# Two small SBUF copies per step of a decoder layer, issued by ScalarE in place of SyncE

## The chip, the cores and the metric

The kernel runs on one core of a Trainium2 chip. The metric is the device time of one execution in microseconds; the kernel before has a median of 670.93 us over 3 runs (668.68 to 674.22).

## The reference

One post-norm decoder layer in float32 on 32 sequences of 64 tokens with 256 channels. x is (32, 64, 256), the context ctx has the same shape. What is computed, cut to its core:

```python
# 1. causal self-attention, 16 heads of 16 channels, then a layer norm over the sum
qkv = einsum('bsd,od->bso', x, w_project)           # 768 outputs
att = softmax(where(causal, -1e9, q @ k.T / 4))
x   = layernorm(x + (att @ v) @ w_out.T)
# 2. cross-attention along the other axis: channels = 64, time = 256, 8 heads of 8 channels,
#    rotary positions on q and k, 256 x 256 scores for each of the 8 heads
q, k, v = Wq x + bq, Wk ctx + bk, Wv ctx + bv
p   = softmax(rope(q) @ rope(k).T / sqrt(8))
x   = layernorm(x + Wo (p @ v) + bo)
# 3. feed-forward with 8-bit activations and ternary weights, 256 -> 1024 -> 256
h   = layernorm(gelu(silu(bitlinear(x, w1, b1)))) * g + b
x   = layernorm(x + bitlinear(h, w2, b2))
```

## The kernel before, in words

Two sequences of 64 tokens fill the 128 partitions and make a pair; there are 16 pairs. Phase A (self-attention and cross-attention) is followed by two phases for the feed-forward part, which the change does not touch.

**Phase A as a pipeline.** After a prologue for the first pairs, every engine runs `body(i)` sixteen times, written out in full (bodies 0 to 15 for pairs 0 to 15). A body has 16 steps s, one for each of the 16 score tiles of pair i's cross-attention (for each of its 2 sequences 8 tiles, of two heads and one half of the 256 positions each). Beside those tiles, body i carries other pairs along: the projections and scores of self-attention of pair a = i+3, and the second half of self-attention, its norm and the rotary projections of pair j = i+2. Bodies 14 and 15 have no pair j left (`rotary` is false), bodies 13 to 15 no pair a. The order of the work on each engine is written out by hand; engines are tied together by semaphores alone.

**The cross-attention tiles.** For the softmax each row's maximum is needed before the exponential is taken. TensorE therefore computes each score tile twice: `max_head` (L531) 14 tiles ahead, for VectorE's maxima `MX` (L907), and `exp_head` (L559) with two more contraction rows that hold the negated maximum (in two bfloat16 parts), so that ScalarE's exponential `exp_tile` (L729, out `PB`) gets the difference from TensorE. The operands are `QA` and `KA`: 48 rows of q and k in three bfloat16 parts, and rows 48 and 49 of each half of `QA` for the maxima. `pv_quad` (L574) then multiplies `PB` with the values. `exp_head` of tile n waits for the exponential of tile n-2; `pv_quad` m waits for the exponentials up to 2m+1.

**How the maxima come into the rows.** For each of the two sequences b of a pair: VectorE negates the 8 tiles' maxima into `NM` (L918, L920), TensorE transposes them (`max_transpose`, L545) into a PSUM bank, ScalarE copies that to `MR` (`mt_copy`, L723), and `max_rows` (L356 to L361) waits for that copy and issues two DMAs of 4 KB from `MR` to rows 48 and 49 of the two halves of `QA` (L360). `exp_ready` makes the first `exp_head` of that sequence (tile 0 for b = 0, tile 8 for b = 1) wait for both. `mt_copy(i, 1)` stands at step 3 of body i on ScalarE, directly ahead of the exponential of tile 4 and of `pt_copy(j)`; `mt_copy(i+1, 0)` stands at step 12, ahead of `square_sum` and the exponential of tile 13. There are 32 such copies, so 64 such DMAs.

**What pair j goes through in body i.** TensorE transposes the self-attention probabilities at step 4 (`transpose_p`, L474; its bank is the one that `mt_copy` reads, so it waits for that), ScalarE copies them (`pt_copy`, L709, two instructions), TensorE multiplies with the values at step 5 (`self_pv`, L487), ScalarE copies (`ao_copy`, L716), TensorE projects at step 6 (`out_proj`, L496), VectorE and GpSimd do the layer norm (Y L869, mv L873, rs L295 and L297, X L880), TensorE projects the rotary q at step 9 (`rotary_proj("q")`, L508), VectorE rotates (L888), and GpSimd splits the result into three bfloat16 parts (`split_parts`, last operation L841).

**SyncE's queue.** SyncE (SP) issues every DMA, in this order in body i: loads of pair i+4 and i+3 (L315, L310), `max_rows(i, 1)`, `store_parts("k", j)` (the parts go to DRAM, L330) and `expand_rows("k", j)` (back into `KA` with the heads on other partitions, four DMAs, L343), the load of the context (L321), `store_parts("q", j)`, `max_rows(i+1, 0)`, `expand_rows("q", j)` into `QA`, and `cross_values(a)` (L353). `expand_rows` waits until the store has landed. `max_head` of pair i+1 begins at step 2 of body i and waits there for that pair's `expand_rows` of q and k; those were issued in the body before.

Of the kernel before, what the change touches and what calls it, by code (L numbers as in the profile page):

```python
# [39 lines left out]
HALF, HH = 64, XH // 2  # L40
ROW_M = 6 * XC
# [32 lines left out]
def build_layer(nc, x, xT, ctx, wpT, woT, xW, xB, rows, w1T, w2T, attn_tables, rotary_tables, out):  # L74
    with ExitStack() as outer:
        es = outer

        def sb(name, shape, dt=F32):
            return es.enter_context(nc.sbuf_tensor(name, shape, dt))
# [4 lines left out]
        def sem(name):  # L84
            return es.enter_context(nc.semaphore(name))

        def event(name, steps=1):
            return Event(sem(name), steps)
# [65 lines left out]
        QA = sb("QA", [P, 6, HH, D], BF16)  # L154
# [4 lines left out]
        MR = sb("MR", [32, P], BF16)  # L159
# [37 lines left out]
        mrow = [[sem(f"mrow{p}{b}") for b in range(2)] for p in range(3)]  # L197
        mx_ps, mx_red, negm = event("mx_ps", 16), event("mx_red", 16), event("negm", 4)
        mt_ps, mt_sb = event("mt_ps", 2), event("mt_sb", 2)
# [8 lines left out]
        def wait(eng, ev, pair, step):  # L208
            eng.wait_ge(ev.sem, ev.at(pair, step))  # L209
# [5 lines left out]
        def has(pair, back):  # L215

            return not isinstance(pair.v, int) or pair.v >= back
# [88 lines left out]
        def _(sp):  # L306
            def load_x(a):
                if has(a, 2):
                    wait(sp, ln1, a.plus(-2), 1)
                sp.dma_start(X[:, a.p, :], x[bass.ds(a.v, 1)].rearrange("o p d -> (o p) d")).then_inc(ld_x[a.p], 16)  # L310

            def load_xT(a):
                if has(a, 2):
                    wait(sp, vs_ps, a.plus(-2), 1)
                sp.dma_start(XT[:, a.p], xT[bass.ds(a.v, 1)].rearrange("o p k t -> (o p) k t")).then_inc(ld_xT[a.p], 16)  # L315

            def load_c(j):
                if has(j, 2):
                    wait(sp, xv_ps, j.plus(-2), 1)
                    wait(sp, ro_ps["k"], j.plus(-2), 1)  # L320
                sp.dma_start(C[:, j.p, :], ctx[bass.ds(j.v, 1)].rearrange("o p d -> (o p) d")).then_inc(ld_c[j.p], 16)  # L321

            def store_parts(n, j):

                if has(j, 2):
                    sp.wait_ge(expand[n][j.plus(-2).ring], NEXPAND * (j.plus(-2).rounds + 1))
                wait(sp, split[n], j, 5)
                dst = parts_hbm[n][j.p].rearrange("t r x -> r t x")
                for slots, parts in (((0, 2), (0, 2)), ((2, 4), (1, 3))) if n == "q" else (((0, 3), (0, 3)), ((3, 4), (1, 2))):
                    sp.dma_start(dst[:, slice(*slots)], part[n][:, slice(*parts)]).then_inc(stored[n][j.p], 16)  # L330

            def expand_rows(n, j):

                if has(j, 3):
                    wait(sp, e_ps, j.plus(-3), 16)
                sp.wait_ge(stored[n][j.p], NSTORE * (j.uses + 1))
                dst = {"q": QA, "k": KA}[n]
                for e in range(2):
                    src = parts_hbm[n][j.p].rearrange("t (e c w) x -> e c t (w x)", e=2, c=XC)[e]
                    first = src[:, 0:1].broadcast_to([XC, 3, 2 * HH * D]) if n == "q" else src[:, 0:3]  # L340
                    for g, group in enumerate((first, src[:, 1:4])):
                        low = HALF * e + 3 * XC * g
                        sp.dma_start(dst[low:low + 3 * XC, 2 * j.ring:2 * j.ring + 2].rearrange("p b h x -> p (b h x)"),  # L343
                                     group).then_inc(expand[n][j.ring], 16)

            def cross_values(a):

                if has(a, 1):
                    wait(sp, ao_ps, a.plus(-1), 1)
                wait(sp, vs_sb, a, 1)  # L350
                for b in range(2):
                    src, dst = slice(SEQ * b, SEQ * b + SEQ), slice(SEQ - SEQ * b, 2 * SEQ - SEQ * b)
                    sp.dma_start(VM[dst, b].rearrange("p (j e f) -> p j e f", e=2, f=SD)[:, :, 1 - b],  # L353
                                 VS[src, :].rearrange("p (j e f) -> p j e f", e=2, f=SD)[:, :, 1 - b]).then_inc(crossed, 16)

            def max_rows(i, b):  # L356
                wait(sp, mt_sb, i, b + 1)
                for e in range(2):
                    low = HALF * e + ROW_M
                    sp.dma_start(QA[low:low + 2, 2 * i.ring + b].rearrange("m h (u t) -> m (h u) t", u=2),  # L360
                                 MR[16 * e:16 * e + 16, :]).then_inc(mrow[i.ring][b], 16)  # L361

            p0, p1, p2 = (Pair(0, a) for a in range(3))
            sp.dma_start(wp[:], wpT.rearrange("(k p) n -> p k n", p=P)).then_inc(ld_wp, 16)
            load_xT(p0)
# [24 lines left out]
            store_parts("q", p1)  # L390
            load_c(p2)
            expand_rows("q", p1)
            max_rows(p0, 0)
            sp.dma_start(w1f[:].rearrange("p (k n) -> p k n", k=2), w1T.rearrange("(k p) n -> p k n", p=P)).then_inc(ld_ffn, 16)
            sp.dma_start(w2f[:].rearrange("p (k n) -> p k n", k=8), w2T.rearrange("(k p) n -> p k n", p=P)).then_inc(ld_ffn, 16)

            def body(i, selfs=True, rotary=True, last=False, more=True):
                if more:
                    load_xT(i.plus(4))
                if selfs:  # L400
                    load_x(i.plus(3))
                max_rows(i, 1)
                if rotary:
                    store_parts("k", i.plus(2))
                    expand_rows("k", i.plus(2))
                    if selfs:
                        load_c(i.plus(3))
                    store_parts("q", i.plus(2))
                if not last:
                    max_rows(i.plus(1), 0)  # L410
                if rotary:
                    expand_rows("q", i.plus(2))
                if selfs:
                    cross_values(i.plus(3))
# [263 lines left out]
        def _(act):  # L678
# [39 lines left out]
            def mt_copy(i, b, g):  # L718
                wait(act, mt_ps, i, b + 1)
                before = i.plus(b - 1)  # L720
                if b == 1 or has(i, 1):
                    act.wait_ge(mrow[before.ring][1 - b], NMROW * (before.rounds + 1))
                nc.scalar.activation(MR[:, :], g_b[g][0:32, 0:64].bitcast(BF16), ACT.Copy).then_inc(mt_sb.sem, 1)  # L723

            def exp_tile(i, n):
                wait(act, e_ps, i, n + 1)
                if has(i, 1) or n >= 4:
                    act.wait_ge(pv.sem, 8 * i.v + n // 2 - 1)
                nc.scalar.activation(PB[:, n % 4].rearrange("p e t -> p (e t)"), e_b[n % 2][:, :], ACT.Exp,  # L729
                                     scale=XC ** -0.5).then_inc(e_sb.sem, 1)  # L730
# [9 lines left out]
            def x_keep(a):  # L740
                wait(act, ln1, a, 6)
                nc.scalar.activation(XALL[:, bass.ds(a.v, 1), :], X1[:].unsqueeze(1), ACT.Copy).then_inc(ln1.sem, 1)
# [13 lines left out]
            p0, p1, p2 = (Pair(0, a) for a in range(3))  # L756
# [14 lines left out]
            x_keep(p1)  # L771
            self_exp(p2)
            mt_copy(p0, 0, 1)

            def body(i, first=False, selfs=True, rotary=True, last=False):
                a, j = i.plus(3), i.plus(2)
                for s in range(16):
                    exp_tile(i, s)
                    if s == 0 and not first:
                        u_copy(i.plus(-1), 1)  # L780
                    if s == 0 and selfs:
                        qk_copy(a)
                    if s == 3:
                        mt_copy(i, 1, 1)
                    if s == 4 and rotary:
                        pt_copy(j)
                    if s == 5 and rotary:
                        ao_copy(j)
                    if s == 6 and not first:
                        at_copy(act, i.plus(-1), 1)  # L790
                    if s == 8 and rotary:
                        x_keep(j)
                    if s == 8:
                        u_copy(i, 0)
                    if s == 13 and not first:
                        square_sum(act, i.plus(-1))
                    if s == 11 and selfs:
                        v_copy(a)
                    if s == 12 and not last:
                        mt_copy(i.plus(1), 0, 1)  # L800
                    if s == 15 and selfs:
                        self_exp(a)
                    if isinstance(i.v, int) and i.v == 13 and s in (7, 9):
                        weight_sum((s - 7) // 2)
                    if isinstance(i.v, int) and i.v == 14 and s in (1, 3):
                        weight_round((s - 1) // 2)
# [651 lines left out]
```

## Time and profile before

| | |
|---|---|
| Median of 3 runs | 670.93 us |
| The profiled execution | 677.3 us |
| Its span, first to last instruction | 675.4 us |
| Phase A, about | 0 to 495 us |
| Busy share TensorE / VectorE / ScalarE / GpSimd | 73% / 77% / 56% / 47% |
| Mean granted TensorE clock | 0.829 |
| `QA<-MR` | 64 DMAs of 4.0 KB, all issued by SyncE |

The page gives busy time by engine, the span in 40 slices, DMA queues, the chain that ended last, and the costliest groups of instructions. Busy shares are averages over phases with different limits. The issue of a DMA is not counted as busy on the engine that issues it, and no engine but SyncE issues any here. In a timeline, each line is the start in us, the length in us, the engine, the line of the kernel, the operation, out<-in with the shape, the count, and in square brackets the idle time of that engine just ahead of it with what ended it. PE is TensorE, PEld its weight load, DVE VectorE, ACT ScalarE, POOL GpSimd, SPq SyncE's queue.

### The profile page before, as it was taken

The page shows a single profiled execution, that of the slowest core. Times are in us where ns is not written, and L with a number is a line of the kernel's source. Part 1 is how long each engine was busy: PE and PEld are TensorE (multiplying, and loading weights), DVE is VectorE, ACT ScalarE, POOL GpSimd, SP SyncE. Part 2 cuts the span into 40 slices and gives each one's busy share as a digit, 9 for nine tenths or more (in the row PEclk, how much of TensorE's full clock was granted, in tenths as well). Part 3 has the DMA queues.
Part 4 walks back from the last instruction along what each step waited for, and adds up shares of the span by engine and source line. Part 5 has one row for each costly group of instructions (what it writes and reads, how often), then busy time and mean ns, then how long its engine had stood idle before and what let it go on. Part 6 is the DMA issues. An engine that isn't in the chain of part 4 may idle for free. (4 is left out here: it accounts for less than half of the span.)

```text
span 675.4 us, 12183 instructions
## 1 busy us (share of the span) xinstructions
PE 490.2 (73%) x3986; PEld 253.3 (38%) x4002; DVE 522.3 (77%) x1045; ACT 378.3 (56%) x681; POOL 319.9 (47%) x383
## 2 busy tenths in 40 slices
PE   5556888889888888898898888788966414545445
PEld 3332435444444344444443444333222103333333
DVE  6476678978988879889888898778437677888885
ACT  1211346555556555555565656477548958677673
POOL 6442435364464553644645537320020057776773
PEclk9787779999999999999999999878567955555555
DMA  7212522212222223132222221220000000000000
GB/s 260 59 43 74 177 67 65 68 51 74 75 65 62 64 68 83 49 76 69 72 60 66 66 77 49 51 71 4 1 0 1 0 0 8 16 16 23 16 17 32
DMA packets 51400, 37.04 MB, mean 55 GB/s; under 512 B 21392, under 2 KB 47376, under 8 KB 51216
## 3 DMA queue, kind: packets, MB, share of 16 engines
q1 hardware_dynamic: 51344, 36.33, 18.8%
q8 instruction: 31, 0.51, 0.3%
q14 instruction: 25, 0.20, 0.1%
HBM read 24.52 MB, written 10.49 MB: 52 GB/s over the span
## 5 line engine op out<-in xcount | busy, mean ns | idle before, releaser
L729 ACT ACTIVATE PB<-e_b 128x512 f32<-128x512 f32 x256 | 149.5, 594 | 115.7 <-PE e_b L559 115.3
L907 DVE TENSOR_REDUCE MX<-mx_b 128x2 f32<-128x512 f32 x256 | 171.4, 681 | 44.0 <-PE mx_b L531 43.2
L531 PE MATMUL mx_b<-KA,QA 48*128 48x256 bf16 x512 | 101.3, 287 | 15.0 <-DMA QA<-parts_q 8.4
L559 PE MATMUL e_b<-QA,KA 50*128 50x256 bf16 x512 | 99.5, 289 | 9.6 <-DMA QA<-MR 7.4
L574 PE MATMUL u_b<-PB,VA 128*32 128x256 f32 x1024 | 88.7, 420 | 4.2 <-ACT PB L729 4.1
L823 POOL TENSOR_TENSOR SP<-SP,srec 128x1024 f32<-128x1024 f32 x14 | 26.6, 1901 | 101.4 <-DVE srec L864 101.4
L531 PEld LDWEIGHTS mx_b<-KA,QA 48*128 48x128 bf16 x512 | 31.5, 96 | 96.3 <-DVE MX L907 41.9
L1325 PE MATMUL r_b<-att_tab,Q 128*128 128x128 f32 x128 | 31.5, 427 | 37.5 <-ACT Q L1249 37.4
L818 POOL TENSOR_TENSOR KM<-QK,att_tab 128x1024 f32<-128x1024 f32 x30 | 57.0, 1904 | 1.6 <-ACT QK L684 1.6
L1317 PE MATMUL z_b<-w2q,Q2T 128*128 128x256 bf16 x128 | 30.2, 417 | 37.0 <-ACT Q2T L1272 26.3
L295 POOL TENSOR_TENSOR rs<-mv,epsc 128x1 f32<-128x1 f32 x32 | 6.1, 190 | 96.2 <-DVE mv L283 66.6
L1282 POOL TENSOR_TENSOR rsh<-mvh,epsc 128x1 f32<-128x1 f32 x16 | 15.2, 949 | 56.9 <-DVE mvh L1345 56.9
L1325 PEld LDWEIGHTS r_b<-att_tab,Q 128*128 128x128 f32 x128 | 25.1, 223 | 45.2 <-ACT Q L1249 38.1
L1292 POOL TENSOR_TENSOR N<-N,row_tab 128x1024 f32<-128x1024 f32 x16 | 37.6, 2349 | 1.9 <-ACT N L1256 1.9
L559 PEld LDWEIGHTS e_b<-QA,KA 50*128 50x128 bf16 x512 | 30.0, 96 | 20.1 <-DMA QA<-MR 11.1
L574 PEld LDWEIGHTS u_b<-PB,VA 128*32 128x32 f32 x1024 | 21.2, 112 | 40.4 <-ACT PB L729 25.6
L443 PE MATMUL g_b<-XT,wp 128*128 128x128 f32 x224 | 32.1, 303 | 5.7 <-DMA XT<-in_xT 5.7
L1317 PEld LDWEIGHTS z_b<-w2q,Q2T 128*128 128x128 bf16 x128 | 16.6, 141 | 49.3 <-DVE stz L1363 24.9
L443 PEld LDWEIGHTS g_b<-XT,wp 128*128 128x128 f32 x224 | 29.3, 211 | 11.0 <-DMA wp<-in_wpT 5.7
L462 PE MATMUL g_b<-KM,QK 128*64 128x512 f32 x112 | 30.2, 618 | 3.3 <-issue 3.3
L880 DVE TENSOR_SCALAR X<-Y,mv,rs 128x256 f32<-128x256 f32 x16 | 27.3, 1707 | 5.4 <-POOL rs L297 5.4
L831 POOL TENSOR_TENSOR full_k<-rot_k 128x256 f32<-128x256 f32 x16 | 11.6, 726 | 39.6 <-DVE rot_k L888 39.6
(197 smaller groups left out, 1125.4 us busy)
## 6 DMA issues: line engine op xcount, KB each, us to landing
KA<-parts_k SPq DMA_DIRECT2D x64, 96.0 KB
QA<-parts_q SPq DMA_DIRECT2D x64, 96.0 KB
parts_q<-part_q SPq DMA_DIRECT2D x32, 128.0 KB, 1.9
parts_k<-part_k SPq DMA_DIRECT2D x16, 192.0 KB, 2.1
XT<-in_xT SPq DMA_DIRECT2D x16, 128.0 KB, 2.4
X<-in_x SPq DMA_DIRECT2D x16, 128.0 KB, 2.2
C<-in_ctx SPq DMA_DIRECT2D x16, 128.0 KB, 2.1
out_y<-O SPq DMA_DIRECT2D x16, 128.0 KB, 1.7
```

What stands on the lines that cost most here:

```text
L443: last = nc.tensor.matmul(ps[:, P * c:P * c + P], wp[:, k, P * c:P * c + P], XT[:, a.p, k, :], start=k == 0, stop=k == 1)
L462: last = nc.tensor.matmul(ps[SEQ * b:SEQ * b + SEQ, :], QK[:, c, SEQ * b:SEQ * b + SEQ], KM[:, c, :, SEQ * b:SEQ * b + SEQ], start=False, ...
L531: m = nc.tensor.matmul(mx_b[n % 2][:, D * k:D * k + D], QA[low:low + K_MAX, 2 * i.ring + b, h, P * u:P * u + P], KA[low:low + K_MAX, 2 * i ...
L559: m = nc.tensor.matmul(e_b[n % 2][:, D * k:D * k + D], KA[low:low + K_EXP, 2 * i.ring + b, h, P * sc:P * sc + P], QA[low:low + K_EXP, 2 * ...
L574: last = nc.tensor.matmul(u_b[b][32 * j:32 * j + 32, D * s4:D * s4 + D], VA[:, i.p, sc, b, 4 * s4 + j, :], PB[:, (2 * m + j % 2) % 4, j // ...
L729: nc.scalar.activation(PB[:, n % 4].rearrange("p e t -> p (e t)"), e_b[n % 2][:, :], ACT.Exp, scale=XC ** -0.5).then_inc(e_sb.sem, 1)
L818: ops.tensor_tensor(KM[:, c], QK[:, 2 + c, :].unsqueeze(1).broadcast_to([P, 8, P]), kmask.unsqueeze(2).broadcast_to([P, 8, P]), ALU.mult). ...
L880: nc.vector.tensor_scalar(X1[:], Y1[:], mv1[:, 0:1], rs1[:, 1:2], ALU.subtract, ALU.mult).then_inc(ln1.sem, 1)
L907: nc.vector.tensor_reduce(MX[:, b, e, 2 * q:2 * q + 2, u], mx_b[n % 2][:, :].rearrange("p (e s) -> p e s", e=2), AXL.X, ALU.max).then_inc( ...
L1292: nc.gpsimd.tensor_tensor(N[:, k.p, :], N[:, k.p, :], gam, ALU.mult).then_inc(zg.sem, 1)
L1317: m = nc.tensor.matmul(z_b[j.p][:, 0:D], Q2T[:, j.p, k, :], w2q[:, k, :], start=k == 0, stop=k == 7)
L1325: t = nc.tensor.transpose(r_b[j.p][:, P * k:P * k + P], Q2[:, j.p, P * k:P * k + P], ident)
```

## The change

`max_rows` is no longer in SyncE's program. The same function, with the same two DMAs, the same wait for `mt_sb` and the same semaphore, stands in ScalarE's program, and is called directly behind each `mt_copy`: in the prologue, at step 3 for (i, 1), and at step 12 for (i+1, 0). The bytes, the addresses and TensorE's waits are unchanged.

```diff
 # SyncE
-            def max_rows(i, b):
-                wait(sp, mt_sb, i, b + 1)
-                for e in range(2):
-                    low = HALF * e + ROW_M
-                    sp.dma_start(QA[low:low + 2, 2 * i.ring + b].rearrange("m h (u t) -> m (h u) t", u=2),
-                                 MR[16 * e:16 * e + 16, :]).then_inc(mrow[i.ring][b], 16)
...
             expand_rows("q", p1)
-            max_rows(p0, 0)
...
-                max_rows(i, 1)
                 if rotary:
                     store_parts("k", i.plus(2))
...
                     store_parts("q", i.plus(2))
-                if not last:
-                    max_rows(i.plus(1), 0)
                 if rotary:
                     expand_rows("q", i.plus(2))
 # ScalarE
+            def max_rows(i, b):
+                wait(act, mt_sb, i, b + 1)
+                for e in range(2):
+                    low = HALF * e + ROW_M
+                    act.dma_start(QA[low:low + 2, 2 * i.ring + b].rearrange("m h (u t) -> m (h u) t", u=2),
+                                  MR[16 * e:16 * e + 16, :]).then_inc(mrow[i.ring][b], 16)
...
             mt_copy(p0, 0, 1)
+            max_rows(p0, 0)
...
                     if s == 3:
                         mt_copy(i, 1, 1)
+                        max_rows(i, 1)
...
                     if s == 12 and not last:
                         mt_copy(i.plus(1), 0, 1)
+                        max_rows(i.plus(1), 0)
```

## Rows read from the trace of the kernel before

**Rows 1.** Waits, 123 to 431 us: engine, line, waited for: total us, times, longest.

```profile
PEld mx_b L531 <- DMA QA<-parts_q: 11.5, 12, 2.0
...
PE e_b L559 <- DMA QA<-MR: 6.4, 12, 1.4
```

**Rows 2.** TensorE's timeline, about one body: start us, us, operation, idle before.

```profile
262.16 0.64 PE L574 MATMUL u_b<-PB,VA 128*32 128x256 f32 x8
...
263.60 0.28 PE L559 MATMUL e_b<-QA,KA 50*128 50x256 bf16 x1 [0.36 <-DMA QA<-MR]
...
268.70 0.28 PE L531 MATMUL mx_b<-KA,QA 48*128 48x256 bf16 x1 [1.25 <-DMA QA<-parts_q]
...
272.00 1.06 PE L474 MATMUL g_b<-att_tab,SP 128*128 128x128 f32 x8 [0.47 <-ACT MR L723]
...
273.89 0.69 PE L487 MATMUL g_b<-PT,VM 128*32 128x64 f32 x32
...
280.39 0.70 PE L508 MATMUL g_b<-X,xw_all 128*128 128x256 f32 x2 [1.25 <-DVE X L880]
```

**Rows 3.** ScalarE's timeline, steps 12 to 15 and 3 to 6.

```profile
258.72 0.25 ACT L723 ACTIVATE MR<-g_b 32x128 bf16<-32x128 bf16 x1
...
263.19 0.60 ACT L729 ACTIVATE PB<-e_b 128x512 f32<-128x512 f32 x1 [1.63 <-PE e_b L559]
...
271.60 0.25 ACT L723 ACTIVATE MR<-g_b 32x128 bf16<-32x128 bf16 x1
271.76 0.57 ACT L729 ACTIVATE PB<-e_b 128x512 f32<-128x512 f32 x1
272.66 1.09 ACT L709 ACTIVATE PT<-g_b 128x512 f32<-128x512 f32 x2 [0.33 <-PE g_b L474]
...
274.66 0.38 ACT L716 ACTIVATE AO<-g_b 128x256 f32<-128x256 f32 x1
```

**Rows 4.** Timelines of VectorE and GpSimd: the norm's first step, the last split of q.

```profile
276.32 0.42 DVE L869 TENSOR_TENSOR Y<-g_b,X 128x256 f32<-128x256 f32 x1 [0.70 <-PE g_b L496]
...
259.35 0.67 POOL L841 TENSOR_TENSOR part_q<-full_q,part_q 128x256 bf16<-128x256 f32 x1
```

**Rows 5.** SyncE's timeline: a store and expansion in the prologue, and one body.

```profile
44.29 0.90 SPq L330 DMA_DIRECT2D parts_q<-part_q  x2
46.66 2.85 SPq L343 DMA_DIRECT2D QA<-parts_q  x4
...
260.10 0.89 SPq L330 DMA_DIRECT2D parts_q<-part_q  x2
261.04 1.38 SPq L360 DMA_DIRECT2D QA<-MR  x2
262.52 3.42 SPq L343 DMA_DIRECT2D QA<-parts_q  x4
...
271.88 1.45 SPq L360 DMA_DIRECT2D QA<-MR  x2
274.88 0.91 SPq L330 DMA_DIRECT2D parts_k<-part_k  x2
...
282.52 0.33 SPq L321 DMA_DIRECT2D C<-in_ctx  x1
```

**Rows 6.** Instructions of line 487: who waited for PT (total us, times).

```profile
  PEld g_b L487: 4.0, 15
```

**Rows 7.** Instructions of line 343: ns of one issue, least, median and most.

```profile
L343 SPq DMA_DIRECT2D QA<-parts_q x64: 648/681/1256, 46.7 to 453.9; - x64
```

**Rows 8.** TensorE's timeline in bodies 0 and 14.

```profile
70.98 0.39 PE L559 MATMUL e_b<-QA,KA 50*128 50x256 bf16 x1 [1.03 <-DMA QA<-MR]
...
462.46 0.28 PE L559 MATMUL e_b<-QA,KA 50*128 50x256 bf16 x1 [1.09 <-ACT PB L729]
```

**Rows 9.** Busy us and instructions of PE, PEld, DVE, ACT, POOL; clock; DMA, by stretch.

```profile
71.00:98.00 27.00, 23.73 (x194) 13.20 (x195) 16.89 (x32) 11.93 (x25) 13.19 (x15) 0.80 0.38 127
...
235.00:263.00 28.00, 23.41 (x232) 11.91 (x229) 22.85 (x45) 15.54 (x32) 14.09 (x17) 1.00 0.25 66
```

## The prediction

> **What bounds the kernel now.** I read the waits of phase A first, then the timelines of one body on each engine. The waits say that TensorE stands for a DMA at two places in each of the bodies 2 to 13: at step 0 for `QA<-MR`, and at step 2 for `QA<-parts_q`, the expanded q of the next pair, where its weight loads wait in 12 of 12 bodies, 11.5 us in all [rows 1]. In the body shown these are 0.36 us at 263.60 and 1.25 us at 268.70 [rows 2]. The second is the one that counts, because it closes a loop over the body. Follow pair j: transposes at step 4 (start 272.00), `PT` on ScalarE, `self_pv` at 273.89 [rows 2], `AO` on ScalarE at 274.66 [rows 3], the norm from 276.32, where VectorE had stood idle for TensorE [rows 4], the rotary projection at 280.39, where TensorE stood 1.25 us for the norm [rows 2], rotation and split, then the store and the four expanding DMAs on SyncE [rows 5], whose landing lets TensorE into step 2 of the next body. No link has room: the weight loads of `self_pv` wait for `PT` 15 times [rows 6], and the store starts at 260.10, 0.08 us behind GpSimd's last split, which ends at 260.02 [rows 4, 5]. What lengthens a link lengthens the body; what shortens another path only makes the wait at step 2 longer.
>
> **What leaves SyncE.** Each body loses two pairs of issues there, 1.38 us between the store of q and its expansion (261.04) and 1.45 us ahead of the store of k (271.88) [rows 5]. The second bought nothing: SyncE is free at 273.33 and the store of k starts at 274.88, when its parts are ready [rows 5]. The first lies on the loop, but in the shadow of the store's own landing. In the prologue, with no pair of copies between them, the expansion starts 46.66 - 44.29 = 2.37 us behind the store's start; in the body it is 262.52 - 260.10 = 2.42 us [rows 5]. So 0.05 us a body comes free, 12 x 0.05 = 0.6 us. The expansion of body 13 is not waited for.
>
> **What becomes earlier.** The copy for b = 0 now waits on SyncE from the end of `MR` (258.72 + 0.25 = 258.97) to 261.04 [rows 3, 5], and TensorE pays at step 0. On ScalarE it goes out 2 us sooner and that wait goes. But its 6.4 us over 12 bodies [rows 1] are handed to the wait at step 2, two tiles later, which ends when q has landed: gain nothing. In body 0 there is no wait for q behind it, and its 1.03 us [rows 8] are gained: -1.0.
>
> **What ScalarE takes on, step 12.** Two issues behind `MR`. No DMA issue on ScalarE stands in the trace. Ends: nothing at all below (an issue can't take less); 2 x 0.33 = 0.66 us, SyncE's shortest issue, a context load [rows 5]; 2 x 1.256 = 2.5 us, the longest of line 343 [rows 7]. I take 1.45 us, what the very same two DMAs take on SyncE [rows 5]. The Trainium skill ("Perfetto Trace Analysis", section "DMA Instruction — HWDGE (DVE, Sync)") says that which engines issue such DMAs is policy and the mechanism is the same; no run here shows it yet, and by it the price would be that 1.45. At step 12 it is covered: `MR` ends at 258.97, the issues end near 258.97 + 0.03 + 1.45 = 260.45, the exponential of tile 13 ends by 261.1, and its first user on TensorE is the `pv_quad` at 262.16 [rows 2]; ScalarE then still stands 1.63 us ahead of 263.19 [rows 3]. Nothing, up to a pair of 2.5 us, where about 1 us would show and the wait at step 2 would swallow it.
>
> **What ScalarE takes on, step 3.** Here there is no cover. Behind the issues in ScalarE's program stand the exponential of tile 4, then `PT`, for which TensorE waits. Now: `MR` ends 271.60 + 0.25 = 271.85, the exponential starts at 271.76, overlapping it, and `PT` at 272.66 after 0.33 us idle [rows 3]. Then: SyncE saw the end of `MR` at 271.88 [rows 5], so the two issues run to 271.88 + 1.45 = 273.33; the exponential starts near 273.38; the next start on ScalarE is 0.49 us behind one of this size (two `PT` take 1.09, one exponential 0.60 [rows 3]), so `PT` starts at 273.87. That is 273.87 - 272.66 = 1.21 us late; the idle 0.33 is used up in it, and the overlap lost. `self_pv`, `AO`, the norm, the rotary projection, the store and the landing each follow at once, so the body grows by 1.21 us. `transpose_p` and `PT` run in 14 bodies (0 to 13): 14 x 1.21 = 16.9 us.
>
> **Bodies 14 and 15.** They have no pair j. In body 14 ScalarE is already late (rounding of weights), TensorE waits 1.09 us for an exponential [rows 8], and the issues add to it: +1.5. The copies left, at step 12 of body 14 and step 3 of body 15, I put at +0.4, between 0 and 1.45 each, as ScalarE idles there between tiles.
>
> **Sum.** 16.9 - 0.6 - 1.0 + 1.5 + 0.4 = +17.2 us. The profiled execution took 677.3 us (span 675.4 and 1.9 around it), above the runs' median of 670.93; I carry the difference over: 694.5 for the profiled one, 670.9 + 17.2 = 688 for the median.
>
> **One place where SyncE and ScalarE meet.** ScalarE's issues at step 12 would run from 259.0 to 260.45, and the store of q starts at 260.10 [rows 5]. No two queues issue at a time in this trace, so whether one waits for the other is open: between 0 and 0.35 us a body on the loop (body 0's copy comes behind its store, so 12 bodies), 0 to 4.2 us. I take 0, as no row shows such a wait. The same section of the Trainium skill says that a DMA's issue locks the generator of descriptors for itself, which would make it the 0.35; by the rows the sum is +17.2, by that rule +21.4.
>
> **The rivals.**
> (a) The issue on ScalarE is cheap. With a pair at I us, the body grows by I - 0.24 (1.45 gave 1.21). At I = 0.66 it is 0.42 us: 14 x 0.42 - 0.6 - 1.0 + 0.7 = +5.0, 676; at nothing, -1.6, 669. It stays within 1% for a pair below 0.78 us. For it: nothing shows ScalarE's price. Against it: the same DMA took 0.69 us and more each in every pair shown. About 673.
> (b) The other side, faster: the waits for `QA<-MR` go and do not come back at step 2. Then 6.4 + 1.0 = 7.4 us go, 663.5. It needs both a pair that fits ScalarE's gap at step 3 (0.24 us, free of charge) and a landing of q earlier by 6.4 / 12 = 0.53 us a body; it decides if SyncE's 1.38 us were really what held the expansion. Against it: 2.42 against 2.37.
> (c) The two queues exclude each other, as above: 688.1 + 4.2 = 692.
> (d) TensorE's granted clock falls in the longer bodies. It is 1.00 in the body shown (the 2.4 GHz level throughout) and 0.80 over body 0, the first behind the prologue (part of it at 1.2 GHz); there it was busy 23.73 us for 194 matmuls against 23.41 for 232 [rows 9], 122 against 101 ns each. TensorE's 23.41 us would grow by 0.21 x 23.41 = 4.9 us, of which its waits take a part; half of it over 12 bodies is +29, near 718. Against it: TensorE stays above 80% busy in a body of 28 us.
>
> **How the numbers follow.** Forecast 0.57, (a) 0.17, (b) 0.05, (c) 0.15, (d) 0.06. The predicted time is the forecast's, 688. Low end 676: the forecast with a pair of 0.66; high end 697: (c) at 692, the 3.3 us that the runs of before reach above their median, and 2 for a pair somewhat slower than SyncE's. Left out are most of (a), (b) and (d), about 2 in 10. One per cent (6.7 us) is about what a measurement of this kernel can tell from no change. Slower by over 1%: forecast, (c) and (d), 0.78; within: (a), 0.17; faster by over 1%: (b), 0.05.
>
> **What would show it.** On ScalarE, `PT` some 1.5 us behind `MR`'s end and more (2.0 us in place of 0.81), with the two issues between; TensorE's wait ahead of `self_pv` or its weight loads grown by 1.2 us in each of 14 bodies; no wait for `QA<-MR` at step 0; a longer wait for `QA<-parts_q` at step 2, not a shorter one; the expansion of q still 2.4 us behind its store (2.7 in case (c)). I am wrong if the issues on ScalarE are much shorter than 0.7 us each, or if bodies that start `PT` late do not start their store of q late.

## The result and the profile after

The changed kernel takes 695.51 us (median of 4 runs, 694.25 to 697.66) against 671.39 us for the kernel before (4 runs, 668.68 to 674.22): the ratio is 1.0362, interval 1.0312 to 1.0413, slower by 24 us. The time lies in the range of the prediction, 7.5 us above the forecast.

The profiled execution after took 695.79 us (span 693.9, clock 0.831). The execution of before that the rows ahead come from was a long one, 677.3 us. The unchanged kernel was therefore profiled again with the experiments, 673.34 us (span 671.5), and stretches are compared with that second profile, called the before-again.

ScalarE's timeline around steps 12 and 3 of the changed kernel answers to [rows 3] (ACTq is ScalarE issuing DMAs):

```profile
266.12 0.25 ACT L712 ACTIVATE MR<-g_b 32x128 bf16<-32x128 bf16 x1
266.40 1.30 ACTq L718 DMA_DIRECT2D QA<-MR  x2
267.80 0.60 ACT L725 ACTIVATE PB<-e_b 128x512 f32<-128x512 f32 x1 [1.43 <-issue]
270.59 0.60 ACT L725 ACTIVATE PB<-e_b 128x512 f32<-128x512 f32 x1 [1.30 <-PE e_b L548]
...
278.70 0.25 ACT L712 ACTIVATE MR<-g_b 32x128 bf16<-32x128 bf16 x1
278.98 1.28 ACTq L718 DMA_DIRECT2D QA<-MR  x2
280.36 0.60 ACT L725 ACTIVATE PB<-e_b 128x512 f32<-128x512 f32 x1 [1.41 <-issue]
280.85 1.08 ACT L698 ACTIVATE PT<-g_b 128x512 f32<-128x512 f32 x2
```

A pair of issues takes 1.28 us on ScalarE (1.45 on SyncE in [rows 5]), and the activation behind it starts 1.41 us after the one ahead has ended. At step 3 `PT` starts 280.85 - 278.70 = 2.15 us after `MR` starts; it was 272.66 - 271.60 = 1.06 [rows 3], so it is 1.09 us late. At step 12 the idle time that followed is still 1.30 us long (1.63 in [rows 3]): the pair there was covered.

The chain behind `PT` in the same profile, on TensorE, VectorE and SyncE, answers to [rows 2, 4, 5]:

```profile
282.03 0.69 PE L476 MATMUL g_b<-PT,VM 128*32 128x64 f32 x32 [0.98 <-ACT PT L698]
284.45 0.42 DVE L868 TENSOR_TENSOR Y<-g_b,X 128x256 f32<-128x256 f32 x1 [0.68 <-PE g_b L485]
288.52 0.70 PE L497 MATMUL g_b<-X,xw_all 128*128 128x256 f32 x2 [1.25 <-DVE X L879]
...
295.86 1.04 SPq L330 DMA_DIRECT2D parts_q<-part_q  x2
298.43 2.77 SPq L343 DMA_DIRECT2D QA<-parts_q  x4
```

`self_pv`, which waited for nothing in [rows 2], now waits 0.98 us for `PT`. From there on every link has its old length: `self_pv` to `Y` 2.42 us (2.43 in [rows 2, 4]), `Y` to the rotary projection 4.07 (4.07). The last link has changed: the store's two issues take 1.04 us where they took 0.89, and the expansion starts 2.57 us behind the store's start, not 2.42.

The waits of the changed kernel, 123 to 445 us (engine, line, waited for: total us, times, longest), and one group of its page (busy us, mean ns, idle before and releaser) answer to [rows 1]:

```profile
PEld mx_b L520 <- DMA QA<-parts_q: 13.8, 11, 1.9
PEld g_b L476 <- ACT PT L698: 12.3, 10, 1.2
PE u_b L563 <- ACT PB L725: 6.0, 12, 0.5
```

```profile
L548 PE MATMUL e_b<-QA,KA 50*128 50x256 bf16 x512 | 98.2, 288 | 4.7 <-ACT PB L725 4.5
```

The wait of `exp_head` for `QA<-MR` at step 0 is gone (6.4 us in [rows 1]). In its place TensorE waits 6.0 us for the exponential of tile 15 (`pv_quad`, L563), 0.5 us in each body, and the weight loads at step 2 wait 13.8 us in 11 bodies for the expanded q, not less than the 11.5 in 12 before. The new wait, for `PT`, stands in the middle of the chain.

The same stretches of both kernels, first the before-again, then the changed one: bodies 0 and 1, bodies 2 to 12, body 6 alone, bodies 14 and 15 up to the last `MR`, and from there to the end of phase A, where the feed-forward part's first `QF` starts. The first three are cut at the start of the store of q. Columns as in [rows 9].

```profile
64.18:121.86 57.68, 47.95 (x434) 24.50 (x433) 44.91 (x85) 27.30 (x57) 27.29 (x32) 0.89 0.33 101
121.86:420.55 298.69, 259.10 (x2512) 130.37 (x2508) 253.99 (x485) 168.64 (x353) 155.15 (x187) 1.00 0.25 67
230.82:258.77 27.95, 23.22 (x230) 11.86 (x228) 22.82 (x44) 15.17 (x31) 14.11 (x17) 1.00 0.24 65
450.56:480.64 30.08, 26.33 (x207) 9.24 (x203) 21.98 (x44) 20.09 (x36) 0.74 (x2) 0.68 0.08 24
480.64:496.97 16.33, 9.62 (x92) 3.60 (x92) 5.45 (x17) 8.89 (x20) 3.49 (x3) 0.89 0.00 1
```

```profile
63.41:123.91 60.50, 49.67 (x432) 25.53 (x433) 45.18 (x85) 26.29 (x55) 27.28 (x32) 0.86 0.32 96
123.91:437.43 313.52, 257.49 (x2501) 131.56 (x2508) 255.93 (x485) 166.49 (x352) 154.83 (x187) 0.99 0.23 64
236.92:267.51 30.59, 25.91 (x231) 12.88 (x228) 23.54 (x45) 15.20 (x32) 14.07 (x17) 0.89 0.22 60
467.00:498.78 31.78, 25.45 (x207) 9.23 (x203) 22.05 (x44) 19.82 (x35) 0.74 (x2) 0.70 0.08 23
498.78:518.25 19.47, 12.54 (x92) 4.33 (x92) 5.45 (x17) 9.02 (x21) 3.49 (x3) 0.70 0.00 1
```

Bodies 2 to 12 account for 313.52 - 298.69 = 14.8 us, 1.35 each, and the last two bodies for 1.7 + 3.1 = 4.8. Bodies 0 and 1 differ by 2.8. The eleven bodies are not alike: body 6 has a lower granted clock in the changed kernel (0.89 against 1.00) and is 2.64 us longer than in the before-again, the other ten are 1.22 longer each.

In the last two bodies there is no pair j and no wait for q, and the issues show directly. ScalarE in body 14, where a rounding of weights stands between the issues and the exponentials, then TensorE's wait; then the same in body 15:

```profile
478.80 2.10 ACT L749 ACTIVATE w2f<-w2f,rnd,winv 128x2048 f32<-128x2048 f32 x1 [1.35 <-issue]
...
481.43 0.39 PE L548 MATMUL e_b<-QA,KA 50*128 50x256 bf16 x1 [2.24 <-ACT PB L725]
...
499.06 1.30 ACTq L718 DMA_DIRECT2D QA<-MR  x2
500.47 1.67 ACT L725 ACTIVATE PB<-e_b 128x512 f32<-128x512 f32 x3 [1.44 <-PE e_b L548]
...
501.12 0.39 PE L548 MATMUL e_b<-QA,KA 50*128 50x256 bf16 x2 [1.23 <-ACT PB L725]
```

The 2.24 us are 0.77 at the same instruction of the before-again: 1.47 more. In body 15 the exponential behind `MR` starts at 500.47, 1.69 us after `MR` starts; in the before-again it is 480.79 - 480.64 = 0.15. (The view puts ScalarE's 1.44 us down to TensorE, but those sums, begun at 499.51, take 0.39 us and were there before the issues ended at 500.36.) TensorE then stands 1.23 us for it, and a little later the granted clock falls, where it stays at 1.00 in the before-again. One stretch of each, the before-again first:

```profile
485.00:489.00 4.00, 2.76 (x32) 1.00 (x28) 1.89 (x6) 2.79 (x6) 0.74 (x2) 1.00 0.00 0
```

```profile
506.00:510.00 4.00, 4.00 (x28) 1.32 (x28) 1.13 (x4) 1.37 (x3) 0.00 (x0) 0.51 0.00 0
```

TensorE's same 92 matmuls of the last stretch take 12.54 us in place of 9.62.

### The profile page after: what moved, and what is told of

It is laid out like the page before. It is cut to its first block and busy times, and to the rows that moved or that the text cites. A ratio compares the mean times of both kernels' runs of the same rounds, so it can differ in the third digit from the quotient of the medians.

```text
span 693.9 us, 12183 instructions
## 1 busy us (share of the span) xinstructions
PE 491.9 (71%) x3986; PEld 255.0 (37%) x4002; DVE 519.7 (75%) x1045; ACT 375.4 (54%) x681; POOL 320.1 (46%) x383
## 5 line engine op out<-in xcount | busy, mean ns | idle before, releaser
L563 PE MATMUL u_b<-PB,VA 128*32 128x256 f32 x1024 | 88.3, 418 | 11.2 <-ACT PB L725 11.1
L563 PEld LDWEIGHTS u_b<-PB,VA 128*32 128x32 f32 x1024 | 21.1, 111 | 48.2 <-ACT PB L725 33.8
```

The source lines that it names most:

```text
L563: last = nc.tensor.matmul(u_b[b][32 * j:32 * j + 32, D * s4:D * s4 + D], VA[:, i.p, sc, b, 4 * s4 + j, :], PB[:, (2 * m + j % 2) % 4, j // ...
```

## The experiments

Theory A is the prediction's: the pair of issues on ScalarE at step 3 makes `PT` late, and the loop over the body grows by that. Its rivals, as each expectation puts them, look for the loss elsewhere: in queues that hold each other up, in ScalarE's new wait for its own `MR`, in the clock, in the tail. A ratio is always to the kernel before, run on the same chip.

**The kernel before, unchanged.** It tells how far one profile can be off.

> The kernel before, unchanged, profiled again beside the others, because its first profiled execution (677.3 us) lies 6 us above the median of its runs, and the gap between the two profiled executions (18.5 us) is smaller than that between the medians (24 us). Theory A (the first profile was a long execution): a span near 669 to 671 us, with the missing 5 to 6 us found in bodies whose landing of q or store came late. Theory B (profiled executions of this kernel are longer by themselves): again about 675 us, and the gap that the traces must explain is 18.5 us.

Measured: 671.48 us, 1.0002 (0.9973 to 1.0031). Bodies 2 to 12 took 298.7 us (298.2 in the first profile). The first profile was longer in bodies 0 and 1 (60.41 against 57.68) and from the last `MR` on (19.86 us at clock 0.59 against 16.33 at 0.89). So bodies 2 to 12 of the kernel before agree to half a microsecond in two profiles, and the two ends only to some 3 or 4 us.

**The two halves.** Only the pair of step 3 on ScalarE, or only that of step 12; the other stays with SyncE at its old place.

```diff
 # step 3 alone, against the changed kernel: SyncE
+            max_rows(p0, 0)
...
+                    max_rows(i.plus(1), 0)
 # ScalarE
-            max_rows(p0, 0)
...
-                        max_rows(i.plus(1), 0)
```

```diff
 # step 12 alone, against the changed kernel: SyncE
+                max_rows(i, 1)
 # ScalarE
-                        max_rows(i, 1)
```

> Only the copies at step 3 (b = 1) move to ScalarE; those for b = 0 stay on SyncE between the store and the expansion of q. Theory A (the pair of issues ahead of PT lengthens the loop): PT 2.15 us behind MR in place of 1.06 in 14 bodies, 14 x 1.03 = 14 us and about 2 in bodies 14 and 15: +15 to +17 us, 686 to 688. Theory B (what costs is the meeting of the two queues at the store of q): nothing is left of the loss, 671 to 673.

> Only the copies at step 12 (b = 0) move to ScalarE; those for b = 1 stay on SyncE. Theory A: covered on ScalarE, so PT stays at 1.06 us behind MR; what is left is the store of q, issued in 1.06 us in place of 0.89 with its expansion 2.58 us behind it in place of 2.42: 12 x 0.16 = 2 us, less 1 us at the start of body 0: 0 to +4 us. Theory B (the meeting of the queues, or the second queue itself, is most of the loss): +8 to +20 us.

Measured: step 3 alone 691.99 us, 1.0291 (1.0236 to 1.0346), 20 us slower; step 12 alone 675.50 us, 1.0055 (1.0018 to 1.0091), 3.7 us slower. Together that is the whole change. Bodies 2 to 12 with step 3 alone:

```profile
124.64:435.37 310.73, 261.34 (x2512) 131.90 (x2508) 253.11 (x485) 167.95 (x353) 154.77 (x187) 0.99 0.24 64
```

With step 12 alone the same bodies take 301.42 us, 2.7 more than in the before-again. But all of that lies in one body, body 7, where the granted clock fell (27.42 us in the before-again, 258.77 to 286.19):

```profile
256.74:287.15 30.41, 26.13 (x232) 13.01 (x228) 23.52 (x45) 15.51 (x32) 14.09 (x17) 0.89 0.22 60
```

The other ten together take 271.01 us against 271.27. With step 3 alone, `MR` to `PT` is 2.15 to 2.18 us and the store's issue in most bodies 0.89 as before; with step 12 alone `PT` is on time in all bodies but body 7, and in most the store's issue takes 1.04 to 1.08, its expansion 2.57 to 2.60 behind its start. The two effects are separate, and the first is by far the larger one; that the second makes a body longer by itself is not shown.

**The wait alone.** The kernel before, with ScalarE waiting for its own `MR` at step 3 and issuing nothing.

```diff
 # ScalarE, kernel before
                     if s == 3:
                         mt_copy(i, 1, 1)
+                        wait(act, mt_sb, i, 2)
```

> The kernel before, all DMAs on SyncE, but ScalarE waits at step 3 for the end of its own copy MR, as it must before it issues, and issues nothing. Theory A (the issues are the price): the exponential of tile 4 starts 0.1 to 0.15 us later, within the 0.33 us idle ahead of PT: no change, 670 to 673. Theory B (the wait for its own result is the price): PT late by 0.5 us or more, +7 us or more.

Measured: 670.96 us, 0.9976 (0.9940 to 1.0013): no change. The exponential no longer overlaps `MR`, and `PT` is on time all the same:

```profile
270.64 0.25 ACT L723 ACTIVATE MR<-g_b 32x128 bf16<-32x128 bf16 x1
270.92 0.60 ACT L729 ACTIVATE PB<-e_b 128x512 f32<-128x512 f32 x1
271.69 1.09 ACT L709 ACTIVATE PT<-g_b 128x512 f32<-128x512 f32 x2 [0.18 <-PE g_b L474]
```

So ScalarE's wait is free, and the issue is what costs.

**Half the dose.** Of the two DMAs of step 3 one on ScalarE, one on SyncE; step 12 as before the change.

```diff
 # SyncE, kernel before
-                max_rows(i, 1)
+                max_rows(i, 1, (1,))
 # ScalarE
                         mt_copy(i, 1, 1)
+                        max_rows(i, 1, (0,))
```

> The kernel before, but of the two DMAs at step 3 one is issued by ScalarE and one by SyncE; the copies at step 12 stay on SyncE. Theory A (the time of the issues itself stands ahead of PT, in proportion): one issue is 0.62 us, so PT is late by 1.09 - 0.66 = 0.43 us (0.33 us of idle before PT is the cover), 14 x 0.4 = 6 us and about 1 in bodies 14 and 15: +5 to +9 us, 677 to 681. Theory B (a fixed price for any DMA behind an activation on ScalarE, such as draining it or waiting for its own copy): nearly the whole +20 us of the two issues, 688 and more.

Measured: 680.1 us, 1.0153 (1.0063 to 1.0242), 7.8 us slower. ScalarE's timeline, and bodies 2 to 12:

```profile
273.31 0.25 ACT L723 ACTIVATE MR<-g_b 32x128 bf16<-32x128 bf16 x1
273.59 0.65 ACTq L729 DMA_DIRECT2D QA<-MR  x1
...
274.83 1.08 ACT L709 ACTIVATE PT<-g_b 128x512 f32<-128x512 f32 x2
```

```profile
123.89:427.56 303.67, 257.12 (x2501) 130.69 (x2508) 253.90 (x485) 167.89 (x353) 155.14 (x187) 1.00 0.24 66
```

`MR` to `PT` is 1.52 us, 0.46 late, and the bodies are (303.67 - 298.69) / 11 = 0.45 us longer. One issue more (0.64 us) makes 1.09 late and, with step 3 alone, (310.73 - 298.69) / 11 = 1.09 longer. Body and lateness agree at both doses, to about 0.1 us a body (the links behind `PT` hand on 0.06 us less than its lateness).

**The same issues at other places.** The changed kernel with the step 3 pair behind `ao_copy` at step 5; and the kernel with step 3 alone, with its pair one place later, behind `pt_copy` at step 4.

```diff
 # ScalarE, changed kernel / step 3 alone
                     if s == 3:
                         mt_copy(i, 1, 1)
-                        max_rows(i, 1)
...
+                    if s == 5:     # (s == 4 in the other)
+                        max_rows(i, 1)
```

> Both copies on ScalarE as in the changed kernel, but the pair at step 3 is issued two steps later, behind ao_copy at step 5, where neither PT nor AO stands behind it. Theory A (place, not the engine, is the price): PT back to 1.06 us behind MR, the loop loses only the 0.16 us at the store: within 5 us of the kernel before, 671 to 676; the first exponential of the second half may wait a little for the rows. Theory B (ScalarE has no room for 1.3 us anywhere in a body, as its exponentials feed TensorE): the loss only moves, 685 and more.

> As the kernel with the step 3 copies alone on ScalarE, but with the pair one place later: behind PT, ahead of the exponential of tile 5 and of AO. Theory A (whatever link of the loop stands behind the issues is late by them): PT 1.06 us behind MR again, but AO late by about 0.9 us (issues from 273.8 to 275.1 on the scale of the body shown, the exponential of tile 5, AO at 275.6 in place of 274.66): 14 x 0.9 = 13 us and 2 to 5 in the tail, 684 to 690. Theory B (PT alone matters, because the weight loads of self_pv wait for it): 671 to 675.

Measured: at step 5 675.65 us, 1.0065 (1.0027 to 1.0104), 3.8 us slower than before and some 20 faster than at step 3. At step 4 678.49 us, 1.0150 (1.0095 to 1.0205), 6.7 us slower, where 12 to 18 had been expected. Bodies 2 to 12 at step 5, then ScalarE at step 4:

```profile
120.91:419.43 298.52, 259.35 (x2514) 130.36 (x2512) 255.16 (x485) 167.01 (x352) 154.88 (x187) 1.00 0.25 67
```

```profile
274.12 0.60 ACT L708 ACTIVATE PT<-g_b 128x512 f32<-128x512 f32 x1 [0.33 <-PE g_b L473]
274.56 0.65 ACTq L728 DMA_DIRECT2D QA<-MR  x1
274.62 0.59 ACT L708 ACTIVATE PT<-g_b 128x512 f32<-128x512 f32 x1
275.25 0.62 ACTq L728 DMA_DIRECT2D QA<-MR  x1
...
276.46 0.38 ACT L715 ACTIVATE AO<-g_b 128x256 f32<-128x256 f32 x1
```

With the pair at step 5 the bodies are as long as in the kernel before, though the same issues are on ScalarE. At step 4 the size was missed: the first issue (274.56) runs while the second `PT` (274.62) is still at work, so `AO` comes 2.34 us behind the first `PT` in place of 274.66 - 272.66 = 2.00 [rows 3], about 0.3 us late and not the 0.9 expected. Bodies 2 to 12 take 303.65 us (122.97 to 426.62), 0.45 longer each; 0.33 of it stands in the links behind `PT`, the rest between a store and the next `MR`. At step 3 the issue has to wait for the end of `MR`, and nothing of ScalarE's lies beside it.

**Both pairs in ScalarE's gaps.** Step 5 as above, and the pair of step 12 behind the exponential of tile 14.

```diff
 # ScalarE, on top of the pair at step 5
                     if s == 12 and not last:
                         mt_copy(i.plus(1), 0, 1)
...
+                    if s == 14 and not last:
                         max_rows(i.plus(1), 0)
```

> Both copies on ScalarE, b = 1 behind ao_copy at step 5, and b = 0 behind the exponential of tile 14, so that its issues fall behind the store of q and not into it. Theory A (the queues slow each other's issue only where they meet): the store of q back to 0.89 us and its expansion back to 2.4 us behind it; the rows for b = 0 land about 264.5 on the scale of the body shown, later than the 263.6 of the kernel before, which the wait at step 2 takes up: 670 to 675. Theory B (the second queue slows the store and the expansion wherever its DMAs stand): the store stays at 1.05 us, 674 to 678.

Measured: 679.14 us, 1.0127 (1.0062 to 1.0192), a miss. Bodies 2 to 12 take 297.97 us (121.11 to 419.08), hardly less than before, and the end is long. Its last stretch, and TensorE in body 14:

```profile
479.39:500.17 20.78, 14.94 (x94) 4.76 (x92) 4.62 (x16) 9.26 (x21) 3.50 (x3) 0.58 0.00 1
```

```profile
451.81 0.39 PE L548 MATMUL e_b<-QA,KA 50*128 50x256 bf16 x1 [1.47 <-DMA QA<-MR]
```

The store's issue is back at 0.89 us and its expansion at 2.41, since ScalarE no longer issues beside it. But the later copies let TensorE wait for the maxima, and in bodies 14 and 15 (0.95 us in the latter) no wait for q stands behind to take that in. The last stretch also has a low granted clock (0.58); what share of the loss each of the two has is not shown.

**The tail.** The changed kernel with the last three pairs of copies, those of bodies 14 and 15, back on SyncE.

```diff
 # SyncE
+                if not rotary:
+                    max_rows(i, 1)
...
+                if not rotary and not last:
+                    max_rows(i.plus(1), 0)
 # ScalarE: both calls only
+                        if rotary:
```

> The changed kernel, but the three copies issued in bodies 14 and 15 are back on SyncE. The medians of the steps so far (step 3 alone +20, step 12 alone +3.7) add up to the change's 24, of which bodies 2 to 12 explain about 15. Theory A (the last two bodies cost by themselves, ScalarE's issues there putting off exponentials for which TensorE waits, and TensorE's granted clock behind that): 3 to 6 us come back, 689 to 692, and the stretch from the last copy to the first QF is 16.3 us again in place of 19.5. Theory B (the tail's length is chance, it varies by 3 us between executions of the kernel before too): no change, 694 to 697.

Measured: 687.78 us, 1.0283 (1.0233 to 1.0333). That is 7.7 us below the changed kernel by the medians and 5.3 by the ratios (0.0079 x 671), from three pairs out of 32; the intervals of the two ratios overlap a little. Its bodies 2 to 12, in which its program is the changed kernel's, and its last two windows, cut as those of the changed kernel:

```profile
119.93:431.27 311.34, 257.54 (x2512) 130.59 (x2508) 255.58 (x485) 166.53 (x352) 154.76 (x187) 1.00 0.23 64
460.81:490.97 30.16, 26.16 (x210) 9.28 (x203) 22.03 (x45) 19.84 (x36) 0.74 (x2) 0.69 0.08 24
490.97:507.35 16.38, 9.85 (x92) 3.63 (x92) 5.45 (x17) 8.89 (x20) 3.49 (x3) 0.88 0.01 1
```

The last two are as long as those of the before-again, to 0.1 us. Bodies 2 to 12 take 2.2 us less than in the changed kernel's profile, as no body has the low clock of body 6 there.

**Shortening what the loop does wait for.** SyncE issues the four DMAs that expand q one after the other. Three kernels give some of them to ScalarE behind the exponential of tile 14: two of the four; the last one; and the last one together with the step 12 pair.

```diff
 # SyncE, kernel before
-                    expand_rows("q", i.plus(2))
+                    expand_rows("q", i.plus(2), 3)      # shown: the last of the four on ScalarE
 # ScalarE
+                    if s == 14 and rotary:
+                        expand_last(j)                  # waits for the store, issues the fourth
```

> The kernel before with one change of its own: of the four DMAs that expand q, two (the second half of the partitions) are issued by ScalarE behind the exponential of tile 14, two by SyncE; the copies of the maxima stay on SyncE. Theory A (the loop is closed by the landing of q, which comes 2.3 to 2.7 us behind the last of the four issues): the last issue ends about 1.4 us sooner, the wait at step 2 goes, and bodies 2 to 13 shorten by 0.6 to 1.2 us, about the waits for q of the kernel before: -7 to -13 us, 659 to 664. Theory B (the loop is closed elsewhere, by TensorE itself or by ScalarE): no gain, or a loss as ScalarE waits for the store with exponentials behind it: 671 to 680.

> The kernel before with only the last of the four DMAs that expand q on ScalarE, behind the exponential of tile 14; all copies of the maxima on SyncE. Theory A: q lands 0.7 us earlier, the wait at step 2 falls from about 0.7 to near 0, the wait for the rows (0.4 us) stays and now counts: 0.3 to 0.6 us a body, 665 to 670. Theory B, as above: 670 to 674.

> A kernel meant to be faster than both: the copies for b = 0 on ScalarE at step 12, those for b = 1 on SyncE, and of the four DMAs that expand q the last one is issued by ScalarE behind the exponential of tile 14. Theory A (with two issues there the wait for q went, and a wait for ScalarE's next exponential of 0.68 us and the wait for the rows of 0.41 us took its place; one issue of 0.68 us fits before that exponential): q lands about 0.7 - 0.16 us earlier, no wait for the rows, 0.4 to 0.6 us a body: 664 to 669. Theory B (TensorE or VectorE bounds the body at 26.9 to 27.1 us as soon as q lands earlier): 670 to 674.

Measured: two of four 675.28 us, 1.0054 (1.0023 to 1.0085); one of four 674.11, 1.0027 (0.9983 to 1.0072); with the step 12 pair 671.38, 1.0001 (0.9961 to 1.0041). No gain, where A had expected 7 to 13 us from the first; by its interval that one is even slower. In it TensorE waits only 0.6 us for q from 123 to 431 us, but 8.2 us for ScalarE's exponentials at `pv_quad`, and bodies 2 to 12 take 301.19 us (123.00 to 424.19). The waits of the last of the three, 123 to 431 us:

```profile
PE u_b L573 <- ACT PB L744: 12.0, 12, 1.6
...
PEld mx_b L530 <- DMA QA<-parts_q: 5.6, 12, 1.2
```

The wait for q halves (11.5 us in [rows 1]) and bodies 2 to 12 shorten by 0.2 us each (296.45 us), but TensorE now waits 1.0 us a body for ScalarE's exponential of tile 15 (0.5 in the changed kernel), which the new issue holds up. No version tried beats the kernel before.

## Why the prediction held, and where it did not

**Step 3 of the body: right.** Predicted 1.45 us for the pair and `PT` 1.21 us late, measured 1.28 and 1.09. The links behind hand it on with 0.06 us less, so the loop grows by 1.03 us. Only this place costs so much: at half the dose and at step 4 it is 0.45 us a body, at step 5 nothing, and the wait without the issues nothing. Rival (a), a cheap issue, is excluded by its own bound, a pair below 0.78 us.

**Step 12 of the body: right on ScalarE, wrong on SyncE.** The pair is covered there, as predicted. The 0.6 us from an earlier expansion did not come; it starts 0.16 us later in most bodies, since the store's two issues, which meet ScalarE's, take 0.15 us longer. By the kernels with one half each it is the pair at step 12 that does it. Rival (c) had the queues overlap by 0.35 us; in the body shown they overlap by 266.40 + 1.30 - 267.51 = 0.19, as ScalarE's pair is shorter than 1.45, so the store is longer by most of the overlap. The Trainium skill ("Perfetto Trace Analysis", section "DMA Instruction — HWDGE (DVE, Sync)") says that an issue first waits for a lock on the block that generates the descriptors. The traces agree with that only in part: in body 13 of the changed kernel ScalarE's pair runs beside the whole store, and neither is longer than alone.

```profile
466.81 1.28 ACTq L718 DMA_DIRECT2D QA<-MR  x2
467.00 0.88 SPq L330 DMA_DIRECT2D parts_q<-part_q  x2
```

So why the two delay each other in the other bodies stays open. That the 0.16 us is time lost is not shown either: with the pair at step 5 the expansion starts as late (2.57 us behind the store), and the eleven bodies take what they took before; with step 12 alone ten of the eleven do.

**The wait for `QA<-MR`: right in that it brings nothing, wrong in where it goes.** In the place of its 6.4 us stand 6.0 us of a new wait for tile 15, and only 2.3 us more at step 2 (13.8 against 11.5), where all of it had been put down. Rival (b) got nothing.

**The sum over bodies 2 to 12.** The measured 14.8 us stand against 11 x (1.21 - 0.05) = 12.8 predicted. Ten bodies grew by 1.22 us each, near 1.03 + 0.16 = 1.19, though the second term, as said, is not shown by itself. Body 6 grew by 2.64. It begins with a store of q issued in 1.93 us (1.39 at the same place of the before-again), TensorE waited 1.71 us for q in it, and its clock was 0.89. That is rival (d) in small: once, not in half of the bodies. The body of low clock in the kernel with step 12 alone has a wait of 1.65 us for q; whether the long wait brings the clock down or merely goes with it stays open. It isn't a fixed cost of the change: the same program took 311.34 us for these bodies in the run with its tail on SyncE, 12.65 more than the before-again and close to the 12.8.

**The tail: the step that was mis-sized.** "The copies left", at step 12 of body 14 and step 3 of body 15, were put at +0.4, "as ScalarE idles there between tiles". Body 14 gave the +1.5 foreseen (1.47). But at step 3 of body 15 the issues hold an exponential up by 1.5 us and TensorE by 1.23, and some microseconds later the granted clock is near 0.5 where it had been 1.00. In the traces the tail lost 4.8 us against 1.9 predicted; by the runs with the tail's copies back on SyncE, 5 to 8. So of the 24.1 us against the 17.2 of the sum the tail makes 3 to 6, and bodies 2 to 12 in the profile shown 2.0. How much of the tail is the clock alone can't be told exactly: the first profile of before has that low clock too (19.86 us, 0.59) with all copies on SyncE. The last pair (at step 3 of body 15, at step 4 or 5 in three kernels) is what differs: of nine profiles with at least one of its two DMAs on SyncE that is the only one (the others: 0.86 to 0.90); of the five with both on ScalarE three have it (0.56 to 0.70).

**Bodies 0, 1 and 13: not settled.** Body 0's wait went, yet bodies 0 and 1 took 60.50 us against 57.68 and 60.41 in the two profiles of before, and the same program 58.73 in the run with its tail on SyncE; body 13 took 29.57 against 30.01 and 27.54, so its 1.21 us can't be read there. Both stretches hold a changing clock (0.80 to 0.90). The feed-forward part, which has none of the work, is 1.1 us longer. With the pair at step 5 the runs are 3.8 us slower although the traced bodies are not; that too is left open.

## What to carry to other kernels

The issue of a DMA is work on the engine that issues it, 0.64 us a piece here, so moving it off a queue that has room onto an engine that stands in a loop costs, in each turn, what no idle time there covers (1.09 of a pair's 1.28 us). Before moving one, look for what stands behind it in the new engine's program and whether TensorE waits for that; two places later in the same program, behind the copies that are waited for, the same issues left the loop as long as it had been. That holds for the bodies; that run as a whole was still 3.8 us slower. A wait that goes buys nothing while another wait of the same loop ends later, and the last turns, which lack that second wait, pay in full.

## What the runs showed that was not expected

An issue overlaps an activation that is still at work, if it does not wait for it: with the pair behind `PT` the first one started at 274.56, ahead of the end of the second `PT` at 275.21. In the kernel with the pair at step 5 the issues and `AO` even start at the same time. And the issues on ScalarE, but for the very first, had nearly the same length. The changed kernel first, then the same DMAs on SyncE in the kernel before:

```profile
L718 ACTq DMA_DIRECT2D QA<-MR x64: 620/622/1537, 65.8 to 499.7; - x64
```

```profile
L360 SPq DMA_DIRECT2D QA<-MR x64: 610/682/727, 68.4 to 481.0; - x64
```

Least, median and most are 620, 622 and 1537 ns on ScalarE, and 647 at most without the first; on SyncE they are 610, 682 and 727.
